# Token setup of a fused SSM, attention and MoE kernel: tables on seven powers, exponentials grouped, first chunk in halves

## The chip, the core and the metric

The kernel runs on one core of one Trainium2 chip. The metric is device time in microseconds (us) of one execution. The engines are TensorE (PE, with its weight loads as PEld), VectorE (DVE), ScalarE (ACT), GpSimd (POOL) and SyncE (SP), which issues DMAs. Each engine works through its own list of instructions in order and waits on semaphores that other engines raise.

## The reference

One transformer-like layer is computed: a state-space convolution kernel makes 256 tokens of width 512 for each of 8 batch rows, 128 text tokens are appended, and attention and a mixture of experts follow, each behind a layer norm and with a residual. The change touches only the first part:

```python
dt = jnp.exp(log_dt)                              # (256,)
w = -jnp.exp(log_w_real) + 1j * w_imag            # (256, 64)
dtA = w * dt[:, None]
K = dtA[:, :, None] * jnp.arange(512)
Cm = Cc * (jnp.exp(dtA) - 1.0) / w                # (8, 256, 64)
K = 2 * jnp.einsum('chn,hnl->chl', Cm, jnp.exp(K)).real
h = jnp.concatenate([K, txt], axis=1)
h = h + attn(layernorm(h))
h = h + moe(layernorm(h))
```

So exp(dtA * l) is needed for l = 0..511, 256 channels and 64 states, and is contracted over the states with Cm.

## The kernel before, in words

The 512 powers are written in base 8: l = 64 i + 8 j + k with i, j, k from 0 to 7. For each channel and state there are three small tables of eight powers, "z" (64 dtA i), "w" (8 dtA j) and "b" (dtA k), each with a cosine and a sine part that are scaled by a magnitude exp(real part). Products of the tables give the operands of TensorE. The 128 partitions hold the 64 states twice, once for the real and once for the imaginary part; 256 channels lie along the free axis, so one table is 256 x 8 = 2048 numbers per partition.

The token setup runs once, in this order. DVE makes dt and w's magnitude from one 128x512 tile by a range-reduced exponential with a ScalarE tanh in the middle (L447 to L467), then rho = real part of dtA and the reduced angle R and its multiples for z and w (L469 to L494), then the coefficients (exp(dtA) - 1) / w (L496 to L543). Meanwhile ACT makes the magnitudes of z and w with `Exp` into PSUM (MAG_ZW, L314, eight instructions of 128x512, one per power), then loads the table with `Sin` (L319), and writes the angles of all three tables (TURN, L328 and L326, 24 instructions of 128x256). DVE rounds the angles (L547, L549); ACT makes sine, absolute value and cosine (L333, L334, L336) for the three groups in turn. Then ACT loads the `Exp` table again and makes the magnitude of b (MAG_B, L338). DVE has by then made the token coefficients U and V (L553 to L561) and scales the z and w tables with MAG_ZW (L566, L567); POOL scales the b table with MAG_B (L421, L422). TensorE multiplies two weight matrices into one PSUM bank (L589, the product "WB").

After that come eight chunks of 32 channels. For each, ACT copies the z and w cosines into PSUM (L353, and L357 for w's sine in even chunks), DVE makes P1, in even chunks P2, and G1 (L576, L580, L582, 128x2048 each), POOL makes G2 and in odd chunks P2 (L431, L430), and TensorE runs 128 fp32 products (L607) in two halves of 64, each of which ends in a bank that ACT copies out (L371). Buffers alternate, so DVE and POOL wait for the chunk two back. After the last chunk TensorE turns the result, and compression, attention (softmax `Exp` in L1729) and the expert layers follow. A function `keep_warm` (L1238) exists but nothing calls it. Every instruction's place in an engine's list is the order in which the code is written; nothing is planned at run time.

Of the kernel before, what the change touches and what calls it, by code (L numbers as in the profile page):

```python
# [15 lines left out]
P = 128  # L16
# [15 lines left out]
HALF = N  # L32
# [137 lines left out]
def build(nc, a):  # L170

    with ExitStack() as ctx:
# [48 lines left out]
        MAG_ZW = PS.rearrange("p b x -> p (b x)")  # L221
# [27 lines left out]
        def htile(i, w):  # L249
# [4 lines left out]
            "xk", "xk2", "xf", "xf2", "xnum", "xden", "xrec", "xe", "xbits", "x", "rho", "rho8", "rho64", "s", "k", "k2", "s1", "s2", "s3", "r", "r2"]  # L254
# [5 lines left out]
        set_a = steps("set_a", ["xt", "th", "mag_zw", "sh", "ch"] + [f"t{g}" for g in GROUPS]  # L260
                      + [f"{x}{g}" for g in GROUPS for x in ("sin", "abs", "cos")] + ["mag_b"])
        set_g = steps("set_g", ["wsum", "cos2", "sin2"])
# [3 lines left out]
        tok_v = steps("tok_v", [f"{x}_{n}" for n in CHUNKS for x in (("P1", "P2", "G1") if n % 2 == 0 else ("P1", "G1"))])  # L266
        tok_g = steps("tok_g", [f"{x}_{n}" for n in CHUNKS for x in (("G2",) if n % 2 == 0 else ("P2", "G2"))])
# [7 lines left out]
        XX, XK, XF, XTH = (cut(work, k * H, 2 * H) for k in (0, 4, 6, 8))  # L275
# [30 lines left out]

        def tok_scalar(act):
            act.wait_ge(set_v.sem, set_v.at("xf2"))
# [4 lines left out]
            for j in range(AW):  # L313
                last = act.activation(by_8(MAG_ZW)[:, :, j], RHOB[:, 0:2 * H], ACT.Exp, scale=float(j))  # L314
            last.then_inc(set_a.now("mag_zw"), 1)

# [5 lines left out]
            for g in GROUPS:  # L322
                for j in range(AW):
                    out = by_8(TURN[:, g * Q:(g + 1) * Q])[:, :, j]
                    if g == 2:
                        last = act.activation(out, R, ACT.Identity, scale=float(j), bias=ec("phase"))  # L326
                    else:
                        last = act.activation(out, (RZ, RW)[g], ACT.Copy, scale=float(j))  # L328
                last.then_inc(set_a.now(f"t{g}"), 1)
            for g in GROUPS:  # L330
                part = slice(g * Q, (g + 1) * Q)
                act.wait_ge(set_v.sem, set_v.at(f"gt{g}"))
                act.activation(SIN[:, part], KT[:, part], ACT.Sin, scale=(2 if g == 2 else -2) * SIN_PI).then_inc(set_a.now(f"sin{g}"), 1)  # L333
                act.activation(TURN[:, part], KT[:, part], ACT.Abs).then_inc(set_a.now(f"abs{g}"), 1)  # L334
# [2174 lines left out]
```

## Time and profile before

| what | value |
|---|---|
| time, median of 3 runs | 863.58 us (862.84 to 863.75) |
| span of the profiled execution, first to last instruction | 856.7 us |
| median less span: what lies around the span | 6.9 us |
| PE busy | 745.3 us (87%) |
| DVE busy | 513.0 us (60%) |
| POOL busy | 347.0 us (41%) |
| ACT busy | 309.8 us (36%) |
| token setup up to the first product of chunk 0 | 73.9 us |
| eight chunks on TensorE | 73.9 to 137.0 us |

The profile of the execution gives its span; the times of the runs also hold what lies before the first and behind the last instruction. Shares of busy time are means over stages of very different kinds: in the first 73.9 us TensorE does next to nothing, and behind that it is busy nearly all the time. A stage is therefore read by the chain of waits, which follows the last instruction back to what released it, and by the list of instructions in order of time, where a bracket behind a row tells how long the engine had stood idle and for whom.

### The profile page before, as it was taken

To read this page: it belongs to the slowest core of one execution; us is meant where nothing else is said; L and a number is where in the kernel's file an instruction comes from. 1 tells how busy PE (TensorE), PEld (TensorE's weight loads), DVE (VectorE), ACT (ScalarE), POOL (GpSimd) and SP (SyncE) were. 2 spreads that over 40 slices of the span, in tenths; PEclk is the share of its full clock that TensorE was granted. 3 is DMA by queue.
4 is the path that set the end of the run, shared out by engine and by line. 5 is a ranking of instruction groups with operands and counts; after the bars stand their busy time and mean duration, and the time that the engine had idled before them with its cause. 6 is when DMAs were issued, how large, how long until landed. Compare 5 with 4: busy or idle time off the path is not lost.

```text
span 856.7 us, 18955 instructions
## 1 busy us (share of the span) xinstructions
PE 745.3 (87%) x6717; PEld 465.7 (54%) x6718; DVE 513.0 (60%) x929; ACT 309.8 (36%) x582; POOL 347.0 (41%) x359
## 2 busy tenths in 40 slices
PE   0006999879889999999999999999999999999992
PEld 0006999655436454555545545665665656656551
DVE  7996764867786474856875533554444444444441
ACT  4782432525225253435333412333223223223231
POOL 0027683343065021210037753555545545455432
PEclk9999999999999999999999999999999999999997
DMA  5010225325272314296562528898976777677752
GB/s 213 0 49 27 77 66 181 109 76 103 67 185 37 93 61 140 86 218 149 157 153 51 156 65 207 168 157 129 143 138 120 143 135 131 138 136 129 126 99 37
DMA packets 126894, 99.73 MB, mean 116 GB/s; under 512 B 95889, under 2 KB 96017, under 8 KB 126321
## 3 DMA queue, kind: packets, MB, share of 16 engines
q1 hardware_dynamic: 99344, 43.64, 22.8%
q0 software_dynamic: 14240, 30.06, 19.3%
q10 hardware_dynamic: 13248, 25.17, 10.6%
q8 instruction: 44, 0.72, 0.4%
q14 instruction: 18, 0.14, 0.0%
HBM read 48.46 MB, written 28.15 MB: 89 GB/s over the span
## 4 chain that ended last, share of the span: by engine, by line
PE 72%; DVE 12%; ACT 5%; DMA 4%; POOL 2%; issue 2%; SPq 2%; ACTq 0%; DVEq 0%; POOLq 0%
PE PS L2159 12%; PE PS L2160 12%; PE PS L2161 12%; PE PS L607 7%; PE PS L1105 6%; PE PS L1107 6%; PE PS L1106 6%; PE PS L765 3%; PE PS L2182 2%; SPq L1877 2%; DVE work L1470 1%; DVE big L1465 1%; DMA work<-in_shared 1%; PE PS L1260 1%; DMA big<-x_dram 1%
## 5 line engine op out<-in xcount | busy, mean ns | idle before, releaser
L2159 PE MATMUL PS<-big,work 128*128 x493 | 165.7, 336 | 4.7 <-DMA work<-big 2.7
L2160 PE MATMUL PS<-big,work 128*128 x493 | 165.7, 336 | 0.0
L2161 PE MATMUL PS<-big,work 128*128 x493 | 165.7, 336 | 0.0
L2331 POOL DMA_INDIRECT out_dram<-work x55 | 88.1, 1602 | 120.1 <-DVE work L2299 54.6
L2224 ACT ACTIVATE work<-PS 128x768 f16<-128x768 f16 x55 | 44.6, 810 | 165.5 <-PE PS L2182 165.5
L2273 DVE SCALAR_TENSOR_TENSOR work<-work 128x352 f16<-128x352 f32 x55 | 32.1, 584 | 89.8 <-ACT work L2231 89.8
L1714 POOL DMA_INDIRECT slots_dram<-work x48 | 48.9, 1019 | 81.2 <-DVE work L2075 62.8
L2315 POOL DMA_INDIRECT big<-x_dram,work x55 | 55.5, 1009 | 45.4 <-POOL work L2312 45.4
L2159 PEld LDWEIGHTS PS<-big,work 128*128 128x128 f16 x493 | 48.4, 98 | 39.6 <-issue 6.1
L2161 PEld LDWEIGHTS PS<-big,work 128*128 128x128 f16 x493 | 48.4, 98 | 36.1
L2160 PEld LDWEIGHTS PS<-big,work 128*128 128x128 f16 x493 | 48.3, 98 | 33.4
L1105 PE MATMUL PS<-work,big 128*128 128x384 f16 (+1 forms) x236 | 63.3, 290 | 1.2 <-DMA big<-x_dram 1.2
L1106 PE MATMUL PS<-work,big 128*128 128x384 f16 (+1 forms) x236 | 63.4, 290 | 0.0
L1107 PE MATMUL PS<-work,big 128*128 128x384 f16 (+1 forms) x236 | 63.2, 290 | 0.0
L2299 DVE TENSOR_SCALAR work<-PS,work 128x512 f32<-128x512 f32 x55 | 44.5, 810 | 28.3 <-PE PS L2161 28.3
L607 PE MATMUL PS<-big,work 128*64 128x64 f32 x1024 | 54.8, 226 | 6.6 <-DVE big L582 6.2
L1195 ACT ACTIVATE work<-work 128x384 f16<-128x384 f32 (+1 forms) x48 | 25.0, 521 | 95.5 <-DVE work L1210 95.2
L589 PE MATMUL PS<-big 128*64 128x64 f32 x32 | 2.0, 316 | 65.7 <-DVE big L567 65.7
L1105 PE MATMUL PS<-big 128*128 128x384 f16 x176 | 57.4, 326 | 1.8 <-DVE big L1220 1.8
L2259 DVE SCALAR_TENSOR_TENSOR work<-work,PS 128x352 f32<-128x352 f32 x55 | 28.6, 521 | 49.8 <-PE PS L2161 48.3
L1107 PE MATMUL PS<-big 128*128 128x384 f16 x176 | 57.4, 326 | 0.0
L1106 PE MATMUL PS<-big 128*128 128x384 f16 x176 | 57.4, 326 | 0.0
(286 smaller groups left out, 1680.0 us busy)
## 6 DMA issues: line engine op xcount, KB each, us to landing
big<-in_weights ACTq DMA_DIRECT2D x33, 272.0 KB, 3.5
work<-in_weights ACTq DMA_DIRECT2D x31, 272.0 KB, 3.1
work<-in_shared ACTq DMA_DIRECT2D x28, 256.0 KB, 3.1
x_dram<-big SPq DMA_DIRECT2D x24, 256.0 KB, 2.3
out_dram<-big SPq DMA_DIRECT2D x24, 256.0 KB, 2.9
big<-in_par SPq DMA_DIRECT2D x1, 1185.0 KB, 10.4
big<-in_c_real SPq DMA_DIRECT2D x1, 1024.0 KB, 5.6
big<-in_c_imag SPq DMA_DIRECT2D x1, 1024.0 KB, 7.5
```

The source lines that it names most:

```text
L607: mm = pe.matmul(out, power[:, h * PW:(h + 1) * PW], coeff[:, h * 64:(h + 1) * 64], start=(k == 0), stop=(k == 3))
L1105: pe.matmul(out, a_high, b_high, start=start, stop=False)
L1106: pe.matmul(out, a_high, b_low, start=False, stop=False)
L1107: return pe.matmul(out, a_low, b_high, start=False, stop=stop)
L1714: pool.indirect_dma_start(slots_d, bass.IndirectOffsetOnAxis(ap=IDX[:, k, t:t + 1], axis=0), PAY[:, n, :].bitcast(U32), None).then_inc(s_s ...
L2159: pe.matmul(out, x_high, w_high, start=start, stop=False)
L2160: pe.matmul(out, x_high, w_low, start=False, stop=False)
L2161: return pe.matmul(out, x_low, w_high, start=False, stop=stop)
L2224: act.activation(AT[c % 2], PS[:, TBK, :].bitcast(F16)[:, 0:2 * len(FCH) * P], ACT.Copy).then_inc(m.acopy, 1)
L2299: nc.vector.tensor_scalar(YO[u], PS[:, OB[u], :], AMX[:, u:u + 1], at_tile(SLOTS[:, :, 1], i, t), ALU.mult, ALU.mult).then_inc(routed.y, 1)
L2315: pool.indirect_dma_start(X16[u], None, x2_d, bass.IndirectOffsetOnAxis(ap=G_NUM[u][:, 0:1], axis=0)).then_inc(s_x[u], 16)
L2331: pool.indirect_dma_start(out_d, bass.IndirectOffsetOnAxis(ap=S_NUM[u][:, 0:1], axis=0), YO[u], None, compute_op=ALU.add).then_inc(s_add[u ...
```

## The change

Eight edits, all in the token setup:

1. dt and w's magnitude part ways. ACT takes the plain `Exp` of w's half (EW); DVE's range-reduced exponential stays for dt alone, on 128x256 in place of 128x512. The bits of the power of two (`xbits`) are made while the tanh runs, and one wait between two independent instructions goes.
2. All three tables lose their power 0: every instruction on them handles powers 1 to 7, as 256 runs of seven numbers out of eight in memory. MAG_ZW lies packed, seven per channel, in seven PSUM banks. The constants for power 0 (1 or 0) are written by six POOL memsets at the start.
3. MAG_B is made right behind MAG_ZW, ahead of the `Sin` table; the second load of the `Exp` table in the setup goes.
4. POOL's sum of two weight matrices (`wsum`) waits until DVE has passed step `m2`.
5. TensorE makes WB as soon as its operands are there, not behind the scaled tables; the bank that holds it is no longer part of MAG_ZW.
6. When the z and w tables are scaled, TensorE runs nine 128x128 products of the identity into bank 7 (`keep_warm`, whose bank is now WARM = 7), ahead of chunk 0.
7. Chunk 0 is made in two halves of 16 channels; TensorE's first half waits for the first pieces only. The channels within a chunk are put in another order on the host so that a half of the products needs one half of the pieces.
8. POOL's scaling of the b table waits for its last cosine in place of MAG_B.

```diff
-        MAG_ZW = PS.rearrange("p b x -> p (b x)")
+        MAG_ZW = PS.rearrange("p b x -> p (b x)")[:, 0:2 * H * (AW - 1)].rearrange("p (h a) -> p h a", a=AW - 1)
+        WARM = 7
...
+        def pieces(n):
+            return (("a", 0, HC // 2), ("b", HC // 2, HC)) if n == 0 else (("", 0, HC),)
...
+        def powers(x):
+            return by_8(x)[:, :, 1:AW]
...
+            act.wait_ge(s_dt, 16)
+            act.activation(EW, EW, ACT.Exp).then_inc(set_a.now("ew"), 1)
             act.wait_ge(set_v.sem, set_v.at("xf2"))
             act.activation(XTH, XF, ACT.Tanh, scale=0.5).then_inc(set_a.now("xt"), 1)
...
-            for j in range(AW):
-                last = act.activation(by_8(MAG_ZW)[:, :, j], RHOB[:, 0:2 * H], ACT.Exp, scale=float(j))
+            for j in range(1, AW):
+                last = act.activation(MAG_ZW[:, :, j - 1], RHOB[:, 0:2 * H], ACT.Exp, scale=float(j))
             last.then_inc(set_a.now("mag_zw"), 1)
+            for j in range(1, AW):
+                last = act.activation(by_8(MAG_B)[:, :, j], RHO, ACT.Exp, scale=float(j))
+            last.then_inc(set_a.now("mag_b"), 1)
...
-                for j in range(AW):
-                    out = by_8(TURN[:, g * Q:(g + 1) * Q])[:, :, j]
+                for j in range(1, AW):
+                    out = by_8(group(TURN, g))[:, :, j]
...
+                kt, turn, sin, cos = (powers(group(x, g)) for x in (KT, TURN, SIN, COS))
                 act.wait_ge(set_v.sem, set_v.at(f"gt{g}"))
-                act.activation(SIN[:, part], KT[:, part], ACT.Sin, scale=(2 if g == 2 else -2) * SIN_PI).then_inc(set_a.now(f"sin{g}"), 1)
+                act.activation(sin, kt, ACT.Sin, scale=(2 if g == 2 else -2) * SIN_PI).then_inc(set_a.now(f"sin{g}"), 1)
...
-            for j in range(AW):
-                last = act.activation(by_8(MAG_B)[:, :, j], RHO, ACT.Exp, scale=float(j))
-            last.then_inc(set_a.now("mag_b"), 1)
...
+            act.wait_ge(wb_p.sem, wb_p.at("wb"))
+            act.activation(WB, PS[:, 7, :].rearrange("p (a d) -> p a d", a=AW), ACT.Copy).then_inc(wb_a.now("wb"), 1)
             act.wait_ge(set_v.sem, set_v.at("cos1"))
             tables(0)
             tables(1)
...
+            for name, out, value in zip(FIRSTS, (cos_zw, sin_zw, b1[0:HALF], b1[HALF:P], b2[0:HALF], b2[HALF:P]),
+                                        (1.0, 0.0, 1.0, 0.0, 0.0, 1.0)):
+                pool.memset(out, value).then_inc(set_g.now(f"first_{name}"), 1)
+                pool.wait_ge(set_g.sem, set_g.at(f"first_{name}"))
             pool.wait_ge(s_par, 16)
+            pool.wait_ge(set_v.sem, set_v.at("m2"))
             pool.tensor_tensor(pc("out_res_T"), pc("to_kv"), pc("out_res_T"), ALU.add).then_inc(set_g.now("wsum"), 1)
             pool.wait_ge(set_v.sem, set_v.at("V"))
-            pool.wait_ge(set_a.sem, set_a.at("mag_b"))
-            pool.tensor_tensor(B1, B1, MAG_B, ALU.mult).then_inc(set_g.now("cos2"), 1)
+            pool.wait_ge(set_a.sem, set_a.at("cos2"))
+            pool.tensor_tensor(powers(B1), powers(B1), powers(MAG_B), ALU.mult).then_inc(set_g.now("cos2"), 1)
...
+            v.tensor_scalar(XBITS.bitcast(I32), XK, 127.0, 2.0**23, ALU.add, ALU.mult).then_inc(set_v.now("xbits"), 1)
             act_done("xt")
...
-                v.tensor_scalar(KT[:, part], TURN[:, part], MAGIC, MAGIC, ALU.add, ALU.subtract).then_inc(set_v.now(f"kt{g}"), 1)
+                v.tensor_scalar(kt, turn, MAGIC, MAGIC, ALU.add, ALU.subtract).then_inc(set_v.now(f"kt{g}"), 1)
...
-                v.tensor_tensor(SIN[:, part], SIN[:, part], MAG_ZW[:, part], ALU.mult).then_inc(set_v.now(f"sin{g}"), 1)
+                v.tensor_tensor(sin, sin, mag, ALU.mult).then_inc(set_v.now(f"sin{g}"), 1)
...
+                for k, h0, h1 in pieces(n):
+                    to = [P, h1 - h0, 8, 8]
+                    v.tensor_tensor(grid(P1[u])[:, h0:h1], table(4 + u, HC * 8, h0, h1).unsqueeze(3).broadcast_to(to), fast(B1, n, h0, h1), ALU.mult).then_inc(
+                        tok_v.now(f"P1_{n}{k}"), 1)
...
             pe.wait_ge(wb_a.sem, wb_a.at("c"))
-            pe.wait_ge(set_v.sem, set_v.at("cos1"))
...
             mm.then_inc(wb_p.now("wb"), 1)
+            pe.wait_ge(s_late, 16)
+            pe.wait_ge(wb_a.sem, wb_a.at("wb"))
+            pe.wait_ge(set_v.sem, set_v.at("cos1"))
+            keep_warm(pe, 9)
...
                 for x in range(2):
+                    if x < len(pieces(n)):
+                        k = pieces(n)[x][0]
+                        pe.wait_ge(tok_v.sem, tok_v.at(f"G1_{n}{k}"))
+                        pe.wait_ge(tok_g.sem, tok_g.at(f"G2_{n}{k}"))
...
-                                h = half * 16 + x * 8 + hr
+                                h = x * 16 + half * 8 + hr
```

Three places in the order of the instructions. The first is ACT between the exponentials and the end of the sines; `PS` is the PSUM tile, `big` and `work` are SBUF tiles, and set_v and set_a are the counters of DVE's and ACT's setup steps. Before:

```order
L314 ACTIVATE PS<-work 128x512 [waits set_v]
L314 ACTIVATE PS<-work 128x512 x7
L319 ACT_TABLE_LOAD [waits s_early]
L319 ACTIVATE work<-work 128x256 [waits set_v]
L320 ACTIVATE work<-work,early 128x256
L328 ACTIVATE big<-work 128x256 [waits set_v]
...
L336 ACTIVATE big<-big,early 128x2048 [waits set_a]
L338 ACT_TABLE_LOAD
L338 ACTIVATE big<-work 128x256 x8
L344 ACTIVATE big,early<-big 128x512 [waits set_g,s_par]
```

The same stretch of ACT in the changed kernel:

```order
L337 ACTIVATE PS<-work 128x512 [waits set_v]
L337 ACTIVATE PS<-work 128x512 x6
L340 ACTIVATE big<-work 128x256 x7
L345 ACT_TABLE_LOAD [waits s_early]
L345 ACTIVATE work<-work 128x256 [waits set_v]
L346 ACTIVATE work<-work,early 128x256
L354 ACTIVATE big<-work 128x256 [waits set_v]
...
L363 ACTIVATE big<-big,early 128x256x7 [waits set_a]
L368 ACTIVATE big,early<-big 128x512 [waits set_g,s_par]
```

MAG_B (L338, now L340) stands ahead of the sines with seven instructions in place of eight, and no table load stands behind them any more.

The second place is ACT at the first softmax, in the attention of the first pair of batch rows; at_v counts DVE's steps there (the row maxima), tr_p TensorE's transposes. Before:

```order
L1723 ACTIVATE big<-PS 128x384 [waits at_p]
L787 ACTIVATE big<-PS 128x2x256 [waits tr_p] x2
L1017 ACTIVATE big<-work 128x512 [waits s_stage1]
L990 DMA work<-in_shared 128x512 [waits sp_low]
L787 ACTIVATE big<-PS 128x2x256 [waits tr_p]
L1729 ACTIVATE big,work<-PS,work 128x256 [waits at_v]
L1729 ACTIVATE big,work<-PS,work 128x384
```

And in the changed kernel:

```order
L1761 ACTIVATE big<-PS 128x384 [waits at_p]
L825 ACTIVATE big<-PS 128x2x256 [waits tr_p] x2
L1055 ACTIVATE big<-work 128x512 [waits s_stage1]
L1028 DMA work<-in_shared 128x512 [waits sp_low]
L825 ACTIVATE big<-PS 128x2x256 [waits tr_p]
L1767 ACT_TABLE_LOAD
L1767 ACTIVATE big,work<-PS,work 128x256 [waits at_v]
L1767 ACTIVATE big,work<-PS,work 128x384
```

The table that holds `Exp` is now loaded here, behind a copy of turned tokens (L787, now L825) and ahead of the first `Exp`.

The third place is the start of TensorE's list; tok_v and tok_g count the pieces that DVE and POOL have made for the chunks, wb_a ACT's steps on the weights. Before:

```order
L589 MATMUL PS<-big 64x64 [waits set_v,wb_a]
L589 MATMUL PS<-big 64x64 x15
L607 MATMUL PS<-big,work 64x64 [waits tok_g,tok_v]
L607 MATMUL PS<-big,work 64x64 x3
L607 MATMUL PS<-big 64x64 x4
```

In the changed kernel:

```order
L622 MATMUL PS<-big 64x64 [waits wb_a]
L622 MATMUL PS<-big 64x64 x15
L1279 MATMUL PS<-late 128x128 [waits set_v,wb_a,s_late]
L1279 MATMUL PS<-late 128x128 x8
L646 MATMUL PS<-big,work 64x64 [waits tok_g,tok_v]
L646 MATMUL PS<-big,work 64x64 x3
...
L646 MATMUL PS<-big 64x64 x4
L646 MATMUL PS<-big,work 64x64 [waits tok_g,tok_v]
```

WB (L589, now L622) waits for the weights alone; the nine products of the identity (L1279) wait for the scaled tables; and a second wait stands in the middle of chunk 0, ahead of its second half.

## Rows read from the trace of the kernel before

**Rows 1.** Chain of waits, 0 to 140 us: start, length, engine and line.
```profile
32.73 1.24 DVE big L547
...
53.36 1.28 ACT L338
...
58.76 4.53 POOL big L421
...
67.16 2.29 DVE work L576
...
73.90 24.52 PE PS L607 x768
```
**Rows 2.** In order of time, DVE and ACT, head of the setup: start, length, instruction [idle before].
```profile
3.56 0.43 DVE L447 TENSOR_SCALAR work<-work 128x512 f32<-128x512 f32 x1 [3.56 <-DMA work<-in_dt_w]
...
5.21 0.69 DVE L453 SCALAR_TENSOR_TENSOR work<-work 128x512 f32<-128x512 f32 x1
5.94 0.63 ACT L309 ACTIVATE work<-work 128x512 f32<-128x512 f32 x1 [3.88 <-DVE work L453]
...
7.52 3.35 DVE L460 RECIPROCAL work<-work 128x512 f32<-128x512 f32 x1
...
12.82 0.42 DVE L469 SCALAR_TENSOR_TENSOR work<-work 128x256 f32<-128x256 f32 x1
13.28 0.42 ACT L311 ACTIVATE work<-work 128x256 f32<-128x256 f32 x1 [6.71 <-DVE work L469]
13.28 0.29 DVE L471 TENSOR_SCALAR work<-work 128x256 f32<-128x256 f32 x1
13.49 0.29 DVE L472 TENSOR_SCALAR work<-work 128x256 f32<-128x256 f32 x1
...
21.26 1.75 DVE L501 RECIPROCAL work<-work 128x256 f32<-128x256 f32 x1
```
**Rows 3.** In order of time, POOL and DVE beside each other at 14 us.
```profile
14.09 1.26 POOL L418 TENSOR_TENSOR big<-big 128x512 f32<-128x512 f32 x1 [13.61 <-DMA big<-in_par]
14.14 1.36 DVE L477 TENSOR_SCALAR work<-work 128x256 f32<-128x256 f32 x1
```
**Rows 4.** In order of time, ACT from 13 to 28 us.
```profile
13.81 4.23 ACT L314 ACTIVATE PS<-work 128x512 f32<-128x512 f32 x8
18.06 1.28 ACT L319 ACT_TABLE_LOAD   x1
...
20.13 7.60 ACT L328 ACTIVATE big<-work 128x256 f32<-128x256 f32 x16
```
**Rows 5.** In order of time: one big DVE step, ACT's table copy, POOL's first piece.
```profile
33.99 2.29 DVE L549 TENSOR_TENSOR big<-big 128x2048 f32<-128x2048 f32 x1
...
65.62 0.60 ACT L353 ACTIVATE PS<-big 128x512 f32<-128x512 f32 x1 [4.66 <-DVE big L567]
...
67.21 3.69 POOL L431 TENSOR_TENSOR big<-big 128x2048 f32<-128x2048 f32 x1
```
**Rows 6.** L607 by stretches: PE and PEld busy (instructions), granted clock, DMA.
```profile
77.00:78.00 1.00, 1.00 (x24) 1.00 (x22) 1.00 0.05 16
...
79.00:80.00 1.00, 1.00 (x42) 1.00 (x39) 1.00 0.00 0
```
**Rows 7.** In order of time, ACT: the copies behind the halves of chunk 0.
```profile
79.80 0.60 ACT L371 ACTIVATE big<-PS 128x512 f32<-128x512 f32 x1 [5.02 <-PE PS L607]
83.53 0.60 ACT L371 ACTIVATE big<-PS 128x512 f32<-128x512 f32 x1 [3.13 <-PE PS L607]
```
**Rows 8.** In order of time, PE: three fp32 products of 128x128.
```profile
155.98 0.83 PE L1262 MATMUL PS<-big 128*128 128x128 f32 x6
```
**Rows 9.** In order of time, ACT ahead of the first softmax.
```profile
161.63 0.60 ACT L787 ACTIVATE big<-PS 128x512 f32<-128x512 f32 x1 [1.71 <-PE PS L619]
```
**Rows 10.** Chain of waits, 140 to 230 us.
```profile
162.34 2.84 ACT big L1729 x12
```
**Rows 11.** In order of time, POOL: a memset of 128x512.
```profile
139.51 0.53 POOL L893 MEMSET big<- 128x512 f32 x1
```

More of the change, by code:

```diff
@@ L361, in tok_scalar @@
             tables(1)
-            act.wait_ge(wb_p.sem, wb_p.at("wb"))
-            act.activation(WB, PS[:, 7, :].rearrange("p (a d) -> p a d", a=AW), ACT.Copy).then_inc(wb_a.now("wb"), 1)
             load_norm(act, 0)
@@ L446, in tok_vector @@
             dve.wait_ge(s_dt, 16)
-            v.tensor_scalar(XK, XX, 1 / np.log(2), MAGIC, ALU.mult, ALU.add).then_inc(set_v.now("xk"), 1)
+            v.tensor_scalar(XK, DT, 1 / np.log(2), MAGIC, ALU.mult, ALU.add).then_inc(set_v.now("xk"), 1)
             own()
@@ L461, in tok_vector @@
             own()
-            v.tensor_tensor(XX, XX, XF, ALU.mult).then_inc(set_v.now("xe"), 1)
+            v.tensor_tensor(DT, DT, XF, ALU.mult).then_inc(set_v.now("xe"), 1)
             own()
-            v.tensor_scalar(XTH.bitcast(I32), XK, 127.0, 2.0**23, ALU.add, ALU.mult).then_inc(set_v.now("xbits"), 1)
-            own()
-            v.tensor_tensor(XX, XX, XTH, ALU.mult).then_inc(set_v.now("x"), 1)
+            v.tensor_tensor(DT, DT, XBITS, ALU.mult).then_inc(set_v.now("x"), 1)
+            act_done("ew")
             own()
@@ L544, in tok_vector @@
             for g in GROUPS:
-                part = slice(g * Q, (g + 1) * Q)
+                kt, turn = (powers(group(x, g)) for x in (KT, TURN))
                 act_done(f"t{g}")
-                v.tensor_scalar(KT[:, part], TURN[:, part], MAGIC, MAGIC, ALU.add, ALU.subtract).then_inc(set_v.now(f"kt{g}"), 1)
+                v.tensor_scalar(kt, turn, MAGIC, MAGIC, ALU.add, ALU.subtract).then_inc(set_v.now(f"kt{g}"), 1)
                 own()
-                v.tensor_tensor(KT[:, part], KT[:, part], TURN[:, part], ALU.subtract).then_inc(set_v.now(f"gt{g}"), 1)
+                v.tensor_tensor(kt, kt, turn, ALU.subtract).then_inc(set_v.now(f"gt{g}"), 1)
             dve.wait_ge(s_c, 32)
@@ L562, in tok_vector @@
             act_done("mag_zw")
-            act_done("cos1")
             for g in range(2):
-                part = slice(g * Q, (g + 1) * Q)
-                v.tensor_tensor(SIN[:, part], SIN[:, part], MAG_ZW[:, part], ALU.mult).then_inc(set_v.now(f"sin{g}"), 1)
-                v.tensor_tensor(COS[:, part], COS[:, part], MAG_ZW[:, part], ALU.mult).then_inc(set_v.now(f"cos{g}"), 1)
+                sin, cos, mag = powers(group(SIN, g)), powers(group(COS, g)), MAG_ZW[:, g * H:(g + 1) * H, :]
+                act_done(f"cos{g}")
+                v.tensor_tensor(sin, sin, mag, ALU.mult).then_inc(set_v.now(f"sin{g}"), 1)
+                v.tensor_tensor(cos, cos, mag, ALU.mult).then_inc(set_v.now(f"cos{g}"), 1)
             own()
@@ L1240, in keep_warm @@
             for k in range(n):
-                pe.matmul(PS[:, 7, 0:P], ident, ident, start=True, stop=True)
+                pe.matmul(PS[:, WARM, 0:P], ident, ident, start=True, stop=True)
         def q_tensor(pe, i):
```

77 lines of the change are left out of this document (41 added, 36 removed).

## The prediction

> **What bounds the kernel now.** I read the busy time in slices first: TensorE does almost nothing until 73.9 us and is nearly full afterwards, so anything that lets chunk 0 start earlier moves everything behind it. The chain of waits over the first 140 us [rows 1] then says who keeps TensorE waiting. The reader is to see one unbroken path: DVE alone up to its first angle step at 32.73, DVE beside ACT's sines, ACT's table load at 53.36 and the exponentials of the b table behind it, POOL's two scalings from 58.76, DVE's first big step of chunk 0 at 67.16, TensorE at 73.90. The lists in order of time [rows 2 to 5] give the price of each kind of instruction, and the copies behind the halves of chunk 0 [rows 7] the rhythm of TensorE.
>
> DVE is in fact busy without a gap from 32.73 until the z and w tables are scaled, which is just before ACT's copy at 65.62 [rows 1, 5]. So two paths end close together: DVE at 65.6 and POOL at 67.1. Taking the b exponentials away from POOL's path alone would win 1.5 us; the rest must come from DVE.
>
> **The change part by part.** All times are in the profiled execution's own clock (span 856.7 us; the median of the runs is 863.58, 6.9 more, which I leave as it is).
>
> *Head of DVE (dt alone, 256 wide).* By [rows 2] a tensor_scalar falls from 0.43 to 0.29, a two-input step from 0.69 to 0.42, the tanh from 0.63 to 0.42, the reciprocal from 3.35 to 1.75. On the path are three of the first kind (0.14 each, 0.42), four of the second (0.27 each, 1.07), the tanh (0.21) and the reciprocal (1.60). `xbits` goes beneath the tanh (one 0.43 step and its 0.03 gap, 0.46). The two tensor_scalars after the tanh no longer wait for each other: they can start 0.21 apart, as L471 and L472 do, where 0.46 stood, so 0.25. Sum 4.0 us: rho, 12.82 before, starts at 8.8. The new `Exp` of w's half runs on an ACT that idles until the tanh; at 0.42 it is over by 4.0 us. Its cost is nothing; it would show only if it came out 1 us longer.
>
> *POOL's sum moved behind m2.* In [rows 3] L477, a 256-wide tensor_scalar, takes 1.36 where its kind takes 0.29 [rows 2], and ends as POOL's sum beside it ends. Moved, the sum runs beside the reciprocal L501 (1.75, [rows 2]) and L477 loses 1.07. What the sum does to a reciprocal no row shows: between nothing and the same 1.07. I take nothing, because a reciprocal at 1.75 for 256 elements asks for operands far more slowly than L477. What waits for the sum is ACT's work on the weights, 30 us later.
>
> *The six memsets on POOL.* One of 128x512 takes 0.53 [rows 11]; two such and four of half the width are 2.1 us at the least and 3.2 at the row's price each, plus their waits. They end near 3 to 4 us, DVE starts at 3.56 [rows 2]. Nothing, or up to 0.5 if they hold the first step. I take nothing.
>
> So DVE's first angle step stands at 32.73 - 4.0 - 1.07 = 27.66.
>
> *ACT in the middle.* This looks like a new wait, so I follow it. MAG_ZW starts 4.0 earlier, at 9.8. Seven steps of 4.23/8 take 3.7; seven of MAG_B at (53.36 + 1.28 to 58.6)/8 = 0.5 each [rows 1] take 3.5: the `Sin` load moves only from 18.06 to 17.0 and the angles from 20.13 to 19.0 [rows 4], though DVE is ready 5 us earlier. Seven angles at 7.60/16 = 0.475 end near 22.4 for the first group and 29.2 for the third. DVE needs the first at 27.66 and the third at 33.8. The cover is over 4 us, so MAG_B costs nothing where it now stands.
>
> *Seven powers of eight.* A 2048-wide DVE step takes 2.29 [rows 5]; 1792 wide it loses 256 elements, 0.27. The tensor_scalar at 1.24 [rows 1] goes at twice the rate and loses 0.13. On DVE's path are three of each and four more scalings: 3 x 0.40 + 4 x 0.27 = 2.27. The scalings then end at 65.6 - 5.07 - 2.27 = 58.25. ACT's nine sine steps lose 0.21 each and end near 46, long before DVE asks. That a pattern of short runs keeps its rate is shown for runs of eight (L576 at 2.29 and L371 at 0.60 for 512 [rows 1, 7]), not of seven, and not for a tensor_scalar: its bounds are 1.1 and the 2.02 of a two-input step, up to 2.8 us for the three. I take 1.1. The Trainium skill ("VectorE: DVE Perf Modes", section "Mode 2×_2P") lets an fp32 tensor_scalar keep two results a cycle where the outermost dimension is even; 256 rows are. By that rule the sum stays, and no run here has shown it yet.
>
> *POOL.* V is ready 6.3 earlier than before (5.07 and 1.20), so at 50.5: before, it stood four scalings of 2.2 ahead of 65.6, at 56.8. POOL need not wait for ACT's exponentials any more, which held it until 58.76, and starts at 50.6. They took from 58.76 to 67.1, 8.3; at seven eighths 7.3: done at 57.9, at the old price 58.9. POOL is no longer last. What is late next is DVE's 58.25 plus ACT's copy into PSUM, 0.60 [rows 5]: chunk 0's first step starts at 58.9 (67.16 before). WB moved to an idle TensorE and costs nothing; ACT's copy of it is over at 51.
>
> *Half a chunk first.* Before, three steps of 2.29 stood between 67.16 and 73.90. Now three of half the width: 1.22 each, two of them 1.13 behind the one ahead, 3.5 in all. The first product can start at 62.45. POOL's half piece, some 1.9 of L431's 3.69 [rows 5], is over at 60.3.
>
> *Nine products ahead.* Chunk 0's first half took 73.90 to 79.80, its second 3.73 [rows 1, 7]. In the slow part TensorE did 24 products a us, later 42, both with the granted clock shown as 1.00, the upper of its two levels (2.4 GHz) [rows 6]; it had begun L607 at 73.90 and was at the faster rate from about 78. Three products of L1262 take 0.83 as six overlapping passes, some 0.22 for one more product [rows 8]; nine cost 2.0 us, 4.0 at half that rate, from 58.3: over by 62.3 at the latest, ahead of 62.45. I take it that they use up the slow stretch: bounds 0 and 5.90 - 3.73 = 2.17 gained, I take 2.17. Then chunk 0 ends at 62.45 + 7.46 = 69.9. Chunk 1 has DVE's last piece at 70.2 (second half of chunk 0 by 65.8, then 2 x 2.2), POOL's at 69.6, and starts at 70.25, where it started at 83.53. From there TensorE sets the pace in both kernels. Gain 13.3.
>
> *The table load comes back.* The sines are now the last table, so the first softmax must load `Exp`. Before, ACT ended a copy at 162.23 and began the softmax at 162.34 [rows 9, 10]; a load of 1.28 with its gaps [rows 4] puts that to 163.55: +1.2, on the chain. Bounds: 0, if ACT came free earlier than the row maxima, and 1.2 as worked out; I take 1.2. The Trainium skill ("ScalarE: Activation LUTs", section "What ACT_TABLE_LOAD costs") wants 2.66 us for every switch, 1.28 of load and 1.38 of drain. By that the sum would be 1.4 worse. The trace disagrees: from the end of L314 at 18.04 the first `Sin` stood 1.32 later.
>
> Sum: -13.3 + 1.2 = -12.1, so 863.58 - 12.1 = 851.5 us.
>
> **Rivals.**
> *The nine products don't help.* If the slow stretch belongs to these products and not to TensorE's first microseconds, chunk 0 keeps 5.90 + 3.73 and chunk 1 starts at 72.1: 853.4. For it: the granted clock shows no step there [rows 6]; against: the first half is slow as a block and then no product ever is.
> *The runs of seven lose the double rate.* Three tensor_scalars 0.93 longer, all on DVE's path: 854.3. For it: no row of that shape; against: runs of eight cost nothing elsewhere.
> *The load costs what the skill's page says.* 852.9; the trace's 1.32 stands against it.
> *The lead is waited away later.* Weight pieces are streamed by DMA during attention and a part of the lead could turn into waiting for them. Half of the lead lost would give 857.5. Against: those DMAs are issued by ACT, in its order, and start earlier too.
> *POOL or the memsets block DVE.* The two bounds above, 0.5 and 1.07: up to 853.1.
> *Slower: POOL works run by run.* Should its two scalings of the b table pay for each of 256 runs, they become the end of the setup. Chunk 1 then starts 11.1 (0.05 of wait, 3.5, 7.5) after them, or at 61.7 + T with T their time. Slower than before needs 61.7 + T + 1.2 > 83.53, T above 20.6 where it was 8.3. At T = 25 the time is 868. Against: L431 walks an equally broken pattern at 3.69 [rows 5], below the 4.2 that the two flat scalings take on average.
>
> **How the numbers follow.** Forecast 0.62; the nine products without effect 0.10; the double rate lost 0.08; the dearer load 0.05; the lead waited away 0.10; POOL blocking 0.03; slower 0.02. The forecast's own spread is about 1.2 either way; with the bounds of the unknown costs and the smaller rivals the range is 850.0 to 855.0. Outside lie most of the waited-away case, the slower one and the forecast's tails, under 2 in 10. All cases but the last leave more than 0.2%, 1.7 us, about what a measurement of this kernel can tell from no change: faster 0.97, within 0.01, slower 0.02.
>
> **What would show it.** In the changed profile: rho at 8.8 and the step L477 at 0.29; ACT's `Sin` load at 17.0; the first 1792-wide tensor_scalar at 27.7 taking 1.1; the last z and w scaling over at 58.3 and POOL's b scalings before it; the first L607 product of chunk 0 at 62.5 and both halves 3.7 long; chunk 1 at 70.3; a load of 1.28 ahead of the first softmax, which stands 12.1 earlier than before. Wrong would be the forecast if POOL ended after DVE, if the tensor_scalars took 2 us, if the first half still took 5.9, or if the shift of 12 us shrank behind the attention.

## The result, and the profile after

The changed kernel takes 854.04 us (median of 4 runs, 851.18 to 857.64) where the kernel before, on the same chip, takes 863.66: a ratio of 0.9896, 95% interval 0.9867 to 0.9924, so 9.0 us less by the ratio (6.6 to 11.5) and 9.6 by the difference of the medians. Six more runs of it gave 852.58 to 859.43 and a ratio of 0.9885 (0.9838 to 0.9932), 9.9 us less (5.9 to 14.0). Forecast were 851.5 us and a gain of 12.1: the direction was right and the time lies in the range of 850.0 to 855.0, near its upper end; the gain was forecast 2 to 3 us too large. The profiled execution is the slowest of the first four (857.64, span 855.9), so places are compared here and not spans.

The head, POOL, DVE and ACT in order of time (start, length, engine and line, what), answers to [rows 2 to 4].

```profile
0.79 4.59 POOL L446 MEMSET big<- 128x512 f32 x6 [0.29 <-POOLq L2538]
17.11 1.26 POOL L450 TENSOR_TENSOR big<-big 128x512 f32<-128x512 f32 x1 [11.73 <-DVE work L530]
...
9.59 0.42 DVE L500 SCALAR_TENSOR_TENSOR work<-work 128x256 f32<-128x256 f32 x1
...
10.91 0.29 DVE L508 TENSOR_SCALAR work<-work 128x256 f32<-128x256 f32 x1
...
16.96 1.75 DVE L532 RECIPROCAL work<-work 128x256 f32<-128x256 f32 x1
...
28.44 1.09 DVE L578 TENSOR_SCALAR big<-big 128x1792 f32<-128x1792 f32 x1
...
17.68 1.28 ACT L345 ACT_TABLE_LOAD   x1
```

rho (L500) stands at 9.59, 0.8 later than forecast: the memsets run until 5.38, beside DVE's first two steps, which take 0.58 and 0.62 in the chain below. The old L477, now L508, takes its 0.29; POOL's sum doesn't hurt the reciprocal L532 (1.75); the 1792-wide step keeps its double rate (1.09).

The chain of waits over the first 140 us (start, length, engine, line), answers to [rows 1].

```profile
3.67 0.58 DVE work L480
4.27 0.62 DVE work L482
...
51.23 2.02 DVE big L597
...
57.10 1.94 DVE big L598
59.18 4.18 PE PS L1279 x18
63.36 23.11 PE PS L646 x768
```

POOL is gone from the chain: its second scaling (L454) starts at 55.44 and takes 3.38, so it ends at 58.8, just before DVE's last (57.10 + 1.94) at 59.0. The nine products, which the chain counts as 18 passes, take 4.18 us, and TensorE turns from them to chunk 0 at 63.34. ACT's copies behind the halves of chunks 0 and 1, answers to [rows 7]:

```profile
67.85 0.60 ACT L395 ACTIVATE big<-PS 128x512 f32<-128x512 f32 x1 [0.23 <-PE PS L646]
71.58 0.60 ACT L395 ACTIVATE big<-PS 128x512 f32<-128x512 f32 x1 [3.13 <-PE PS L646]
75.31 0.60 ACT L395 ACTIVATE big<-PS 128x512 f32<-128x512 f32 x1 [0.38 <-PE PS L646]
```

The first copy stands 11.95 earlier than before (79.80) and so does the second (83.53), and that holds through the token stage. Then the first softmax: two lines of TensorE from the trace of before, then ACT and TensorE in the changed kernel (answers to [rows 9, 10]), and a stretch of 10 us (us, busy PE, PEld, DVE, ACT, POOL with their instructions, granted clock, DMA share, GB/s).

```profile
163.87 0.66 PE L1289 MATMUL PS<-late,big 128*128 128x128 f32 x4 [1.41 <-ACT big L1729]
...
167.72 3.79 PE L765 MATMUL PS<-big 64*128 64x64 f32 x64
```

```profile
149.66 0.60 ACT L825 ACTIVATE big<-PS 128x512 f32<-128x512 f32 x1 [1.71 <-PE PS L657]
150.28 1.28 ACT L1767 ACT_TABLE_LOAD   x1
151.58 0.47 ACT L1767 ACTIVATE big<-PS,work 128x256 f32<-128x256 f32 x1
...
153.10 1.04 PE L1327 MATMUL PS<-late,big 128*128 128x128 f32 x4 [2.61 <-ACT big L1767]
...
158.73 4.41 PE L803 MATMUL PS<-big 64*128 64x64 f32 x64
```
```profile
150.00:160.00 10.00, 6.49 (x31) 4.41 (x31) 6.80 (x18) 6.96 (x19) 0.00 (x0) 0.66 0.06 21
```

The load is there at its price: the first `Exp` is 10.76 earlier than before (162.34), 1.2 less than the copies. But TensorE now idles 2.61 us, 1.41 before, and the granted clock, at its upper level (2.4 GHz) until then, falls to the lower one (1.2 GHz): it reads 0.50 from 154 to 160 us and 0.66 in the mean of the stretch, where the trace of before has 1.00 over 150 to 170 us. L803 (L765 before, 167.72) starts 9.0 earlier than before, not 10.8.

### The profile page after: what moved, and what is told of

It reads as the page before. It is cut to its first block, busy times and chain, and to the rows that moved or that the text cites. A ratio compares the mean times of both kernels' runs of the same rounds, so it can differ in the third digit from the quotient of the medians.

```text
span 855.9 us, 19001 instructions
## 1 busy us (share of the span) xinstructions
PE 753.5 (88%) x6735; PEld 469.8 (55%) x6736; DVE 506.8 (59%) x932; ACT 305.3 (36%) x578; POOL 350.2 (41%) x366
## 3 DMA queue, kind: packets, MB, share of 16 engines
q10 hardware_dynamic: 13248, 25.17, 10.8%
## 4 chain that ended last, share of the span: by engine, by line
PE 73%; DVE 13%; DMA 6%; issue 2%; ACT 2%; POOL 1%; another core or an unknown queue 1%; SPq 0%; POOLq 0%; ACTq 0%; DVEq 0%
PE PS L2197 11%; PE PS L2199 11%; PE PS L2198 11%; PE PS L1143 8%; PE PS L1145 7%; PE PS L1144 7%; PE PS L646 7%; PE PS L803 3%; PE PS L2220 2%; DMA work<-big 1%; DVE big L1062 1%; DMA big<-x_dram 1%; PE PS L1298 1%; DVE big L1503 1%; DVE work L1508 1%
## 5 line engine op out<-in xcount | busy, mean ns | idle before, releaser
L1752 POOL DMA_INDIRECT slots_dram<-work x48 | 48.3, 1005 | 89.1 <-DVE work L2113 65.6
L646 PE MATMUL PS<-big 128*64 128x64 f32 x1024 | 53.7, 223 | 0.0
## 6 DMA issues: line engine op xcount, KB each, us to landing
big<-in_par SPq DMA_DIRECT2D x1, 1185.0 KB, 11.3
```

The lines of the kernel that those rows point to most:

```text
L646: mm = pe.matmul(out, power[:, h * PW:(h + 1) * PW], coeff[:, h * 64:(h + 1) * 64], start=(k == 0), stop=(k == 3))
L1752: pool.indirect_dma_start(slots_d, bass.IndirectOffsetOnAxis(ap=IDX[:, k, t:t + 1], axis=0), PAY[:, n, :].bitcast(U32), None).then_inc(s_s ...
```

## The experiments

Theory A: the setup wins 12, the reload costs 1.2, TensorE's longer pause costs clock. Theory B: a part of the lead is waited away later. Theory C: the fall of the clock has nothing to do with the pause. Times of the runs are medians; single runs of one kernel lie 4 to 14 us apart, so an edit worth a microsecond or two is judged by the place it moves, and the medians are given for completeness.

**The changed kernel again** (after_again; no edit).

> The changed kernel as it is, for a second trace and more times. Theory A (the setup's gain of 12.0 us is steady; the fall of the granted clock at the first softmax belongs to the reload and comes every time; what was lost between 382 and 500 us of the profiled run is an accident of that run): the clock falls to 0.50 near 153 us again, L803 behind the softmax starts 9.0 us earlier than before (near 158.7), and the lead from 200 us to the end stays near 7 to 9 us, so a median near 853 with single runs 3 to 6 us apart. Theory B (the lead is waited away in the attention, for weights and slots): the loss of some 8 us between 382 and 500 us stands in this trace too, at the same lines, and no run is faster than 855. Theory C (the fall at 153 us is an accident too): no fall there, L803 near 156.3.

854.76, ratio 0.9885. The first half of chunk 0 ends at 67.55, the first softmax again loads for 1.28, TensorE pauses 2.60, the clock falls (0.83 over 150 to 160 us), L803 starts at 158.24. So far this speaks against C. Against the first trace of before it, too, loses its lead between 440 and 500 us, as B says; but three of its six runs are faster than 855, which B rules out.

**The kernel before again** (before_again; no edit).

> The kernel before as it is, for a second trace: its profiled execution took 856.7 us of span, while its timed runs take 860 to 866. Theory B' (all kernels lose 5 to 8 us between 440 and 500 us through pauses that several engines take together, which the profiled execution of before happened to miss): the second trace has a span of 861 to 864, TensorE is busy less than 10 of 10 us in several stretches between 440 and 500 us, and the lead of the changed kernel against it is 9 to 12 us at every place, to the end. Theory B (only the changed kernel meets a wait there): the second trace again has TensorE full from 430 to 510 us, span near 857.

866.51, ratio 1.0001 (0.9976 to 1.0025), span 867.7. First the trace of before that the prediction read, then its second, by stretches:

```profile
460.00:470.00 10.00, 10.00 (x63) 5.97 (x61) 5.11 (x9) 4.60 (x9) 7.56 (x9) 1.00 0.12 29
...
480.00:490.00 10.00, 10.00 (x61) 5.87 (x60) 6.39 (x11) 3.99 (x7) 7.87 (x8) 1.00 0.58 177
```
```profile
460.00:470.00 10.00, 8.82 (x54) 5.12 (x53) 2.70 (x5) 2.25 (x5) 6.27 (x7) 1.00 0.02 1
...
480.00:490.00 10.00, 6.83 (x21) 2.22 (x22) 2.68 (x4) 3.28 (x6) 5.89 (x7) 0.83 0.59 168
```

The kernel before pauses there as well; the execution that was profiled first had missed it. Against this trace nothing of the changed kernel's lead goes there: by matching instructions of ACT and DVE it is 9.2 us (first trace) and 13.8 (second) at 440 us, and 8.9 and 13.9 at 480. Theory B falls and B' holds in kind, though not in its sizes: the span is 867.7 and not 861 to 864, and the lead of the second trace is above 12.

**The table loaded early** (exp_early).

```
 act.activation(part, part, ACT.Identity, bias=mean)...   # centring
+act.wait_ge(wb_a.sem, wb_a.at("c"))
+act.activation(ec("centre_c"), ec("centre_c"), ACT.Exp)
```

> One more Exp of one column on ACT right behind the centring of the weights (near 49 us, where ACT then idles), so that the table of Exp is loaded there and not ahead of the first softmax. Theory A: no load at the softmax, first Exp near 150.4 where it was 151.58 (1.2 earlier), TensorE idles 1.4 us there instead of 2.6, the granted clock doesn't fall at 153 us, and L803 starts 3.6 us earlier (near 155.2): median 3 to 4 us below the changed kernel, about 850.4. Rival C: the fall of the clock has nothing to do with the reload: 1.2 us alone, about 852.8, and the fall stands near 152. Rival: the load was hidden beside the row maxima: nothing changes.

854.34, ratio 0.9883 (0.9837 to 0.9928).

```profile
49.24 1.28 ACT L384 ACT_TABLE_LOAD   x1
...
151.93 0.66 PE L1329 MATMUL PS<-late,big 128*128 128x128 f32 x4 [1.40 <-ACT big L1769]
153.88 2.04 PE L823 MATMUL PS<-big 128*128 128x512 f32 x2 [1.28 <-ACT big L827]
...
157.19 3.79 PE L805 MATMUL PS<-big 64*128 64x64 f32 x64
```

The load is free at 49 us and TensorE waits 1.40 again; L805 (the old L803) starts 1.05 earlier than in the changed kernel's second trace. The clock falls all the same (L823 at 2.04, not 1.10). Of the 3.6 us that I expected, about the reload's 1.2 came and the clock's part didn't: here it fell behind a pause of 1.4 too.

**The b magnitudes back behind the sines** (mag_b_late; their loop moved down, and POOL's wait with it, from `cos2` to `mag_b`).

> One part of the change undone: the seven exponentials of the b table go back behind the sines, the rest stays as changed. Theory A: ACT's sines end at 46.7 - 3.4 = 43.2 or stay at 46.7 (they wait for DVE), the load of 1.28 and seven steps of 0.49 end near 51.5, POOL's scaling starts there where it started at 51.40, so the setup loses 0 to 0.1 us, chunk 0 stays at 63.3, and the softmax gets its 1.2 us and its clock back, as in exp_early: about 850.4. Rival (the order of the magnitudes is what won the setup): POOL's scalings, now 51.5 + 7.5, end later than DVE's and chunk 0 moves back by a us or more: 853 to 855. Rival C as for exp_early: 1.2 us better alone.

856.45, ratio 0.9900 (0.9863 to 0.9938).

```profile
46.81 1.28 ACT L361 ACT_TABLE_LOAD   x1
48.11 3.50 ACT L361 ACTIVATE big<-work 128x256 f32<-128x256 f32 x7
...
51.75 4.09 POOL L452 TENSOR_TENSOR big<-big 128x1792 f32<-128x1792 f32 x1 [33.38 <-ACT big L361]
```

POOL starts 0.35 later (51.40 changed), still ends beside DVE, and chunk 0 starts at 63.33, as changed. There is no load at the softmax. ACT's copy behind the first half stands at 68.20 (67.85 and 67.55 in the two traces of the changed kernel), which is within what this half varies by, 4.22 to 4.87 us over the nine traces with nine products right ahead of it. So this part of the change won at most 0.4 to 0.7 us in the setup and put 1.2 us onto the attention; the median doesn't show it.

**TensorE filled while it waits for the softmax** (softmax_fill; the reload left in).

```
+if i == 0 and bt == 0:          # bank k of turn_y, already read
+    pe.wait_ge(t.sem, t.at(f"bank{k - 4}"))
+    for _ in range(11): pe.matmul(PS[:, 4 + k % 4, 0:P], ident, ident, ...)
 pe.wait_ge(at_a.sem, at_a.at(f"exp{bt}0_{i}"))
```

> The reload stays; TensorE gets eleven more products of the identity (2.4 us) ahead of its wait for the first softmax, into a bank whose reader is done. Theory A (the clock falls because TensorE idles 2.6 us there): first Exp still near 151.6, the granted clock doesn't fall at 153 us, L1327 takes 0.66 and not 1.04, L803 0.60 of 64 products in 3.8 and not 4.4 us, starting near 156.3: median about 2.4 us below the changed kernel, 851.6. Rival C (the fall is an accident or belongs to something else): the fall stands as before, nothing gained, and up to 0.3 lost if the products run into the softmax.

855.92, ratio 0.9893 (0.9858 to 0.9927).

```profile
150.15 2.62 PE L1331 MATMUL PS<-late 128*128 128x128 f32 x22
152.92 0.66 PE L1336 MATMUL PS<-late,big 128*128 128x128 f32 x4 [0.15 <-ACT big L1776]
...
156.78 3.79 PE L806 MATMUL PS<-big 64*128 64x64 f32 x64
```
```profile
150.00:160.00 10.00, 8.55 (x97) 7.46 (x95) 8.50 (x22) 6.80 (x19) 0.00 (x0) 1.00 0.05 17
```

The clock doesn't fall, although the second pause behind the softmax (1.30 ahead of 154.88) stands here as elsewhere. The old L803 starts 1.46 earlier than in the second trace of the changed kernel, with the softmax where it was. The total doesn't follow, within its spread.

**No warming products** (no_warm; `keep_warm(pe, 9)` to 0) **and chunk 0 whole** (whole_chunk; `pieces` gives one piece).

> The changed kernel without the nine warming products. Theory A (TensorE's first microseconds of dense work are slow, whatever the work is): the first product of chunk 0 still starts at 63.3, the first half takes 5.9 instead of 4.5, chunk 0 ends 1.4 later and everything behind it by 1.4: the products are worth 1.4 us of the 2.17 that were forecast. Rival (they are worth nothing, or delay chunk 0 since they end at 63.36, where its data are ready): first half ends at 67.85 or earlier.

> The changed kernel with chunk 0 in one piece again. Theory A: DVE's three steps of 2.29 end near 66.5 instead of 63.3, so the first product of chunk 0 starts 3.2 later; the warming products, then over 3 us earlier, leave TensorE idle, and the first half takes between 4.5 and 5.9. Chunk 1's data come at the same time as now, so chunk 1 starts 2.5 to 4.5 us later: the halves are worth about 3 us of the setup's 12. Rival (TensorE waits for the second half anyway, so that halves win nothing): chunk 1 unchanged.

858.42, ratio 0.9925 (0.9884 to 0.9966), and 861.59, ratio 0.9950 (0.9915 to 0.9986). Without warming, then whole:

```profile
63.56 0.69 PE L646 MATMUL PS<-big,work 128*64 128x64 f32 x8 [12.28 <-DVE big L615]
...
69.91 0.60 ACT L395 ACTIVATE big<-PS 128x512 f32<-128x512 f32 x1 [2.28 <-PE PS L646]
```
```profile
66.53 0.70 PE L646 MATMUL PS<-big,work 128*64 128x64 f32 x8 [3.18 <-DVE big L615]
...
73.00 0.61 ACT L395 ACTIVATE big<-PS 128x512 f32<-128x512 f32 x1 [5.58 <-PE PS L646]
```

From its first product to ACT's copy the first half takes 6.35 with no products ahead (5.9 expected) and 4.51 or 4.22 behind them (two traces): they are worth 1.8 to 2.1. The granted clock reads 1.00 from 63 to 71 us with and without them, so it doesn't show why the first products are slow. In the kernel before the same half took 5.90 and, in its second trace, 5.22, with WB's products 6.2 us ahead of it; whether moving WB away cost the 0.4 to 1.1 us up to 6.35 was not tried. In one piece chunk 0 starts 3.19 later, as worked out, and its first half takes 6.47: after a pause of 3.18 the warming is lost. The halves are worth 73.00 - 67.85 = 5.15, where 3 were expected; 2 of them come because the halves let the chunk follow the products without a gap.

**Three edits at once** (setup_all): the early table; the memsets moved behind POOL's sum; `keep_warm(pe, 13)` behind `sin1`.

> Three edits on the changed kernel: the table of Exp loaded behind the centring (49 us); POOL's six memsets behind its sum of the weights (18.4 us) instead of first; thirteen warming products behind the sine scaling at 57.1 instead of nine behind the last one at 59.1. Theory A: rho at 8.9 (0.7 earlier), L508 and the reciprocals unchanged, the last scaling at 58.4, first product of chunk 0 at 62.6, its first half 3.73 instead of 4.5: chunk 1 starts 1.5 earlier than changed, the softmax 2.7 earlier: a median about 2 to 3 us below the changed kernel's. Rival (the memsets hold DVE wherever they stand): rho 0.7 earlier but the steps between 18 and 23 us longer by as much. Rival (the clock's falls later in the run decide): the setup wins 1.5, the total doesn't show it, since runs differ by 3 to 6 us.

854.14, ratio 0.9849 (0.9802 to 0.9896).

```profile
17.64 4.57 POOL L451 MEMSET big<- 128x512 f32 x6
...
3.59 0.30 DVE L482 TENSOR_SCALAR work<-work 128x256 f32<-128x256 f32 x1 [3.59 <-DMA work<-in_dt_w]
...
17.97 0.82 DVE L536 TENSOR_SCALAR work<-work 128x256 f32<-128x256 f32 x1
...
63.27 0.45 PE L648 MATMUL PS<-big,work 128*64 128x64 f32 x8 [1.21 <-DVE big L617]
```

DVE's head is 0.67 earlier (rho at 8.92): 0.59 by its two steps that nothing holds, and 0.08 because dt landed earlier (3.59, 3.67 in the changed kernel). L536 gives 0.59 back (0.23 in the changed kernel): the rival on the memsets holds, and chunk 0 starts 0.07 earlier. The longer warming ends at 62.06 and its first half takes 4.22, what nine products gave in the better of two traces.

**POOL's sum without its wait** (wsum_first; `pool.wait_ge(..."m2")` removed).

> The changed kernel with POOL's sum of the weights back where it was, as soon as the weights have landed (near 14 us), without its wait for m2. Theory A (a two-operand POOL step holds DVE's tensor_scalars while it runs, as in rows 3): the sum of 1.26 stands near 14 us beside the tensor_scalar steps L521 and L523, of which one takes about 1.3 instead of 0.29; the first 1792-wide step starts 1.0 later (29.5) and so does chunk 0 (64.3). Rival (rows 3 was the DMA that landed there, not POOL): nothing moves.

860.45 of two runs 14 us apart, which says nothing.

```profile
14.13 1.27 POOL L449 TENSOR_TENSOR big<-big 128x512 f32<-128x512 f32 x1 [8.75 <-DMA big<-in_par]
...
14.27 1.42 DVE L524 SCALAR_TENSOR_TENSOR work<-work 128x256 f32<-128x256 f32 x1
...
29.44 1.10 DVE L577 TENSOR_SCALAR big<-big 128x1792 f32<-128x1792 f32 x1
```

The size is right (29.44, 1.0 later; chunk 0 at 64.34), the step isn't: it is a two-input step that is held here, 1.42 instead of 0.43. So moving the sum was worth 1.0 of the 12.

**The memsets on DVE** (firsts_dve), with the early table.

```
-pool.memset(out, value).then_inc(set_g.now(f"first_{name}"), 1)
+v.memset(out, value).then_inc(set_v.now(f"first_{name}"), 1)   # ahead of dve.wait_ge(s_dt, 16)
```

> Two edits on the changed kernel: the table of Exp loaded behind the centring, and the six memsets on DVE, which waits for dt until 3.6 us anyway, instead of on POOL. Theory A (memsets on POOL hold DVE's tensor_scalars at any place): with none on POOL the first steps take 0.29, L536 0.23, rho stands at 8.9 and the first product of chunk 0 at 62.6, 0.7 earlier than changed, if six memsets fit into the 3.5 us ahead of dt (at 0.5 each, 3.0); the softmax 1.9 earlier. Rival: at 0.76 each they take 4.6 and end at 4.8, so DVE starts 1.2 late and chunk 0 comes 0.5 later than changed.

854.90, ratio 0.9881 (0.9847 to 0.9916).

```profile
1.34 0.48 DVE L478 MEMSET big<- 128x512 f32 x1 [1.34 <-PEq L2539]
...
4.64 0.27 DVE L478 MEMSET big<- 64x256 f32 x1 [0.30 <-issue]
4.94 0.29 DVE L481 TENSOR_SCALAR work<-work 128x256 f32<-128x256 f32 x1
```

The rival came true, by another sum: two memsets take 0.48, four 0.27, and with about 0.3 between them the six end at 4.91; DVE starts 1.3 later than in the changed kernel and chunk 0 stands at 64.03, 0.7 later. Of the three places the first on POOL, as changed, is as good as any. L822 behind the softmax takes 1.10: no fall here, although TensorE paused 1.41.

**The memsets on DVE, the early table and eleven products** (all_fill), **and the early table with five products** (exp_fill5).

> The two edits of the run before and eleven products of the identity while TensorE waits for the first softmax (without the load 1.4 us of waiting: some of them then stand in the way). Theory A: chunk 0 at 62.6, no load at the softmax, no fall of the granted clock there; the eleven products, 2.6 us in all, end 1.2 behind the moment at which the softmax is ready, which costs 1.2 and saves the 1.2 to 1.7 of a fall; the lead behind the softmax is 12 against the kernel before, 0.5 more than with the exponential moved alone. Rival (the falls come anyway, a little later): the products only cost.

> The version that the runs point to: the changed kernel with the table of Exp loaded behind the centring, and five products of the identity (1.2 us) in the 1.4 us in which TensorE then still waits for the first softmax. Theory A: chunk 0 at 63.3 as changed, first Exp near 150.4, the products end before the softmax is ready, no fall of the granted clock between 150 and 165 us, L803 near 155.2: 1.2 us ahead of the changed kernel where it meets no fall and 2.8 where it meets one; the median, if accidents later in the run are alike, about 852.5, and within the spread of single runs (851 to 859) not told from it for certain. Rival (the fall belongs to the softmax's whole stretch, with its second and third pause, and not to the first): a fall of 3.4 us near 153 again.

854.06, ratio 0.9886 (0.9858 to 0.9913), and 853.05, ratio 0.9860 (0.9830 to 0.9889). The second, at the softmax:

```profile
150.19 1.28 PE L1333 MATMUL PS<-late 128*128 128x128 f32 x10
151.76 0.66 PE L1338 MATMUL PS<-late,big 128*128 128x128 f32 x4 [0.29 <-ACT big L1778]
153.71 1.10 PE L826 MATMUL PS<-big 128*128 128x512 f32 x2 [1.29 <-ACT big L830]
...
155.61 3.79 PE L808 MATMUL PS<-big 64*128 64x64 f32 x64
```

The clock falls in neither here. The first has chunk 0 at 64.01, as the run before, and its old L803 at 156.39, 11.33 earlier than before, where 12 were expected. With five products the old L803 starts 2.63 earlier than in the second trace of the changed kernel and 12.11 earlier than before: at this place the 12 us of the setup are whole. Its interval overlaps with that of the changed kernel, so it beats the kernel before for certain and the changed kernel only by its trace.

Taken together: with a pause of 2.6 us at the softmax the clock fell in five traces of five, with 1.4 in four of six (both traces of before among the six: 1.00 in the first, 0.83 over 160 to 170 us in the second), with the pause filled in none of three. Nine of eleven against none of three speaks for the pause as the cause; that 2.6 is worse than 1.4 isn't shown. From the first L1327 to L803 it takes 3.85 without a fall and without products in the way, 5.1 to 5.6 with one: a fall costs 1.2 to 1.8 us up to there, and the trace that the prediction read had none.

Behind L803 much of this difference goes again. Between 180 and 235 us the granted clock falls in every one of the 14 traces, whether it fell at the softmax or not (in the lowest 5 us to between 0.50 and 0.76). ACT's L1093, for one, stands at 238.36 in the kernel before; first its line in the trace of before, then with the table early, then with five products besides:

```profile
238.36 1.67 ACT L1093 ACTIVATE big<-big 128x512 f16<-128x512 f32 x3 [2.74 <-DVE big L1086]
```
```profile
226.55 1.67 ACT L1133 ACTIVATE big<-big 128x512 f16<-128x512 f32 x3 [2.74 <-DVE big L1126]
```
```profile
226.82 1.67 ACT L1136 ACTIVATE big<-big 128x512 f16<-128x512 f32 x3 [2.75 <-DVE big L1129]
```

The lead against before is 11.8 and 11.5 here: exp_early, whose clock fell at the softmax, is ahead of exp_fill5, whose clock didn't. The same step starts at 228.28 and 227.82 in the two traces of the changed kernel (10.1 and 10.5 ahead) and at 227.10 with eleven products and the reload (11.3). So the load's 1.2 us last (11.8 against 10.1 and 10.5); of the fall's cost, filling the pause kept 0.7 to 1.2 us with the reload and nothing without it, with one or two traces of each.

## Why the forecast was right, and where it was off

| step | forecast | measured |
|---|---|---|
| rho | 8.8 | 9.59 |
| L477, now L508 | 0.29 | 0.29 |
| 1792-wide tensor_scalar | 27.7, 1.1 | 28.44, 1.09 |
| POOL's b scalings end | 57.9 | 58.8 |
| DVE's scalings end | 58.25 | 59.0 |
| first product of chunk 0 | 62.45 | 63.34 |
| its first half | 3.73 | 4.51 and 4.22 |
| lead in the token stage | 13.3 | 12.0 (11.2 against the second trace of before) |
| load ahead of the softmax | 1.2 | 1.2 |
| lead behind it, at L803 | 12.1 | 9.0 and 9.5 (9.8 and 10.3 against the second) |
| lead 70 us further on, at L1093, now L1131 | 12.1 | 10.1 and 10.5 (9.4 and 9.9 against the second) |

*Head and POOL's sum.* The prices of the rows held to a few hundredths; what was mis-sized is the memsets, "nothing, or up to 0.5 if they hold the first step". By the row of 0.53 they had to end by 4; the two of 128x512 take 1.01 each and the four of 64x256 0.55 to 0.59, they end at 5.38, and they hold two steps, 0.59 in all by setup_all. I had taken a flat memset's price for a strided one. That POOL's sum doesn't hold the reciprocal was right (1.75); the reason that I gave, its slow reading, no run tests.

Which step is held is told by the Trainium skill ("SBUF — State Buffer", section "SBUF: two separate sides"): a POOL instruction locks a port pair that a DVE step needs if it runs in a two-port mode, and a two-input DVE step is held only by a POOL instruction that reads SBUF. The runs agree: beside memsets the tensor_scalars stretch (0.57, 0.60; 0.82 for L536) and the two-input L484 doesn't (0.43); beside the sum, which reads, the two-input L524 takes 1.42. With this rule at hand the bound would have been all the time that the memsets still run once DVE has started.

*Seven powers, POOL, half chunks.* Right, each within 0.1 us once the head's 0.8 is taken off; POOL is 0.2 us ahead of DVE, the margin that the sum gave it being 0.35. No run undoes the narrower head or the seven powers; their worth is read from places alone: DVE's scalings end 6.6 us earlier (65.6 before), 3.2 by the head, 1.1 by POOL's sum and 2.3 by the seven powers.

*Nine products.* The mechanism is right, the size was off: I gave the whole 2.17 and took 3.73, which is the distance of two copies in the steady pace, for a length that begins with TensorE's first product. From there a half takes 4.22 even if it starts warm (setup_all). The nine products took 4.18 us, above the bound of 4.0, and ended at 63.36, not by 62.3 "at the latest"; they held nothing up, since chunk 0 starts no earlier without them (63.56).

So in the first trace chunk 0 starts 0.89 late (0.59 by the memsets, 0.11 because dt landed at 3.67 and not 3.56, the rest in small pieces) and its first half is 0.78 too long (0.49 in the second trace), 1.67 together. The forecast had 0.34 us of waiting ahead of chunk 1 that didn't come (ACT's copy at 75.31 follows the one at 71.58 by the usual 3.73). The difference is the 1.3 us that the lead in the token stage lacks.

*The load.* Right to the hundredth: from the end of the copy at 150.26 to the first `Exp` 1.32. What I left out stands behind it: TensorE's pause grows from 1.4 to 2.6, and behind a pause there the clock mostly falls. "1.2, on the chain" was the wait alone; the clock behind it had no term in the sum, and no reason was given for that.

*The lead waited away later*, the rival at 0.10, didn't happen. It looked as if it had as long as one execution of before was the measure. That execution (span 856.7, where the shortest span of a timed run of before is 859.1) had missed pauses of several us that every other trace has. Of the 6.9 us that I put around the span only 1.8 lie there (857.64 against a span of 855.9, 869.49 against 867.7); the other 5.1 are what this execution was faster by than the median. Its places were good all the same: up to 440 us it lies within 2 us of the second trace.

The sum as measured, up to L803: 12.0 - 1.2 - 1.2 to 1.8 for the clock = 9.0 to 9.6 against a trace of before that had no fall there; up to L1131: 10.1 and 10.5. The ratios give 9.0 (6.6 to 11.5) and 9.9 (5.9 to 14.0), which can't tell these apart. All three misses, the memsets, the first half and the clock, made the gain smaller than forecast; the range held because it reached 3.5 us above the forecast and only 1.5 below.

## What to carry to other kernels

An engine that is made to wait longer can be charged twice if TensorE waits behind it: look at what the granted clock does in the rows behind each of TensorE's pauses. A few idle products there kept it up in three traces of three, but look some way further on before counting the gain: here part or all of it was gone 70 us later. A table of ACT that is needed late can be loaded by one dummy column in any idle stretch; before a block is moved to save a load, look where the next load goes. And where a profiled span differs from the median by more than the effect, profile the old kernel twice before reading a difference of late places.

## What the runs showed of the hardware that was not expected

Between 440 and 510 us, in 13 traces of 14, TensorE is idle for 5.4 to 7.2 of the 70 us, and several engines pause at once for which the trace names no releaser: in the second trace of before DVE waits 6.59 and 8.37 us ahead of 467.67 and 485.25, POOL 2.09 and 2.58, put down to "remote", TensorE up to 1.05 a time to "issue", with DMA at 0.02 busy over 460 to 470. The first trace of before alone has none of it. What causes it wasn't tried.

A memset of 128x512 takes POOL 0.53 flat [rows 11] and 1.01 with a stride of eight numbers; one of 64x256 with that stride takes 0.55 to 0.59. DVE takes 0.48 and 0.27 for the strided two, with 0.2 to 0.4 to the next.
